# Attention over 64 heads on one core: score tiles spread over the whole head, their own three PSUM banks, and a new written-out order on all engines

## The reference, cut to what matters

```python
def ttt_filter(scores):
    int_scores = (jnp.abs(scores) * 1618.0).astype(jnp.int32)
    mod9 = int_scores % 9
    chaos = (mod9 == 0) | (mod9 == 3) | (mod9 == 6)
    return scores * jnp.where(chaos, 1 / PHI, 1.0)

def qrt_damping(x):
    return jnp.sin(C1 * x) * jnp.exp(-(x * x) / PHI) + jnp.cos(C2 * x)

scores = jnp.einsum('bhqd,bhkd->bhqk', q, k) / 8.0
attn = jax.nn.softmax(ttt_filter(scores), axis=-1)
attn = attn * qrt_damping(attn)
ctx = jnp.einsum('bhqk,bhkd->bhqd', attn, v)
```

## Time and profile before

| | |
|---|---|
| time, median of 3 runs | 7027.4 us (7016.34 to 7040.62) |
| profiled execution: its time / its span | 7039.49 us / 7037.8 us |
| busy in the span: PE, DVE, ACT, POOL | 81%, 64%, 60%, 39% |
| mean granted TensorE clock | 0.894 of full speed |

### The profile page before, as it was taken

The page is one execution under the profiler, slowest core; times in us unless marked ns, Lnnn a source line. Parts: engine busy times, 40 slices in busy tenths (PEclk is TensorE's granted clock), DMA queues, the critical chain, the costliest instruction groups (busy, mean ns, idle before and its releaser), DMA issues. The chain is left out here.

```text
span 7037.8 us, 110191 instructions
## 1 busy us (share of the span) xinstructions
PE 5716.5 (81%) x28905; PEld 3244.8 (46%) x28905; DVE 4477.5 (64%) x9249; ACT 4254.5 (60%) x7370; POOL 2765.9 (39%) x2640
## 2 busy tenths in 40 slices
PE   2788887887788787888788877788788699997999
PEld 1344443434444343444444334444444377775777
DVE  1766677677666667677766667667766555555443
ACT  1677777677777777777777777777777422222222
POOL 3444444444444444444444444444444301100111
PEclk9888889899888989888888999888888799998989
DMA  1000000000000000000000000000000000000000
GB/s 17 11 7 7 7 7 7 7 7 7 7 10 7 7 7 7 7 7 7 7 7 10 7 7 7 7 7 7 7 7 7 8 1 1 1 1 12 4 5 5
DMA packets 34512, 48.56 MB, mean 7 GB/s; under 512 B 24473, under 2 KB 24537, under 8 KB 34010
## 3 DMA queue, kind: packets, MB, share of 16 engines
q1 hardware_dynamic: 31962, 43.49, 2.4%
q0 software_dynamic: 2048, 0.14, 0.1%
HBM read 39.40 MB, written 4.19 MB: 6 GB/s over the span
## 5 line engine op out<-in xcount | busy, mean ns | idle before, releaser
L587 PE MATMUL banks<-ident,att 128*128 128x128 f32 x8192 | 1492.0, 313 | 644.9 <-DVE ag L523 633.2
L587 PEld LDWEIGHTS banks<-ident,att 128*128 128x128 f32 x8192 | 1044.0, 162 | 1483.8 <-DVE ag L523 1173.9
L388 POOL TENSOR_TENSOR sinb<-sinb,ag 128x512 f32<-128x512 f32 x1024 | 1289.4, 1274 | 1041.6 <-ACT sinb L453 1039.4
L615 PE MATMUL banks<-kT,qT 128*128 128x512 f32 x2048 | 1233.1, 687 | 344.1 <-DVE mx L550 189.8
L398 POOL TENSOR_SCALAR wgt<-wgt 128x512 f32<-128x512 f32 x1024 | 703.4, 687 | 1693.5 <-DVE wgt L516 1688.2
L489 DVE TENSOR_TENSOR work<-banks,work 128x512 f32<-128x512 f32 x1024 | 704.8, 690 | 907.2 <-ACT work L447 854.8
L653 PE MATMUL outp<-work,vo 128*64 128x512 f32 x2048 | 1105.8, 628 | 4.1 <-ACT att L435 4.1
L653 PE MATMUL outp<-sinb,vo 128*64 128x512 f32 x2048 | 1105.9, 628 | 0.0
L471 ACT ACTIVATE mag<-banks 128x512 f32<-128x512 f32 x1024 | 601.8, 594 | 552.7 <-PE banks L615 551.5
L464 ACT ACTIVATE work<-banks 128x512 f32<-128x512 f32 x1024 | 610.3, 596 | 372.9 <-PE banks L587 357.0
L453 ACT ACTIVATE sinb<-banks 128x512 f32<-128x512 f32 x1024 | 606.5, 597 | 312.8 <-PE banks L602 312.8
(11 more groups left out here) (200 smaller groups left out, 7252.1 us busy)
## 6 DMA issues: line engine op xcount, KB each, us to landing
xq<-xT_dram SPq DMA_DIRECT2D x64, 256.0 KB
xv<-xT_dram SPq DMA_DIRECT2D x64, 256.0 KB, 3.7
xT_dram<-xT SPq DMA_DIRECT2D x8, 256.0 KB, 2.9
out<-hres SPq DMA_DIRECT2D x8, 256.0 KB, 2.6
base<-in_L_tok_turns,idx POOLq DMA_INDIRECT x64, 2.3
wqk<-in_L_attn_Wq SPq DMA_DIRECT2D x64, 16.0 KB
wqk<-in_L_attn_Wk SPq DMA_DIRECT2D x64, 16.0 KB
wqk<-in_L_attn_bq SPq DMA_DIRECT2D x64, 0.2 KB
```

The source lines that it names most:

```text
L388: nc.gpsimd.tensor_tensor(sinb[:, k % RING], sinb[:, k % RING], ag[:, k], ALU.mult).then_inc(tmul, 1)
L587: mm = nc.tensor.matmul(bank[:, i * P:(i + 1) * P], att[:, p, 4 * half + i, kt * P:(kt + 1) * P], ident[:], is_transpose=True, start=(i == ...
L615: nc.tensor.matmul(score_bank(n), qT[:, p, (n // 2) * P:(n // 2 + 1) * P], kT[:, (n % 2) * 512:(n % 2 + 1) * 512], start=True, stop=True). ...
```

## The change

The tables hold other numbers, and the banks and two buffers are dealt out differently.

```diff
-        xq = sb("xq", [D + 1, S])
-        xv = sb("xv", [D + 1, S])
+        x = sb("x", [D + 1, S])
-        kT = sb("kT", [P, S])
+        kT = sb("kT", [P, 2, S])
...
-        SCORE = [5, 7, 9, 11] + list(range(12, 24))
-        ABS, RND, KEEP, FACT, FILT = (1, 1, 2, 2, 3)
-        PROJ, VAL = 24, 29 + STEPS
-        EXP = STEPS + 3
+        SCORE = [0, 1, 2, 5, 6, 13, 16, 19, 20, 23, 26, 27, 32, 33, 36, 40]
+        ABS, RND, FACT, FILT, BIAS = 1, 1, 2, 3, 4
+        EXP = [STEPS + o for o in [4, 5, 7, 8, 9, 10, 12, 16]]
...
         def score_bank(n):
-            return banks[:, n % 4]
-        def gauss_bank(d):
-            return banks[:, 4 + d % 3]
-        def sine_bank(k):
+            return banks[:, n % 3]
+        def turn_bank(k):
             return banks[:, 3 + k % 4]
...
-                wait(sp, projd, 2 * t)
+                if isinstance(t, int):
+                    wait(sp, projd, 2 * t)
+                else:
+                    wait(sp, vald, t - 2)
...
-                        if a in SCORE:
-                            n = SCORE.index(a)
-                            wait(pe, filtered, NTILE * g + n - 3)
-                            if n == 3:
-                                wait(pe, sined, NTILE * (g - 2) + 13)
...
-                        j = a - EXP - PACE
-                        if 0 <= j < TB:
-                            wait(pe, expd, TB * g + j + 1)
...
+                            wait(pe, filtered, NTILE * g + (n - 2 if n >= 3 else (0, -2, -1)[n]))
```

More of the change, by code:

```diff
@@ L351, in load_v @@
             def load_v(t):
-                wait(sp, vald, t)
-                sp.dma_start(xv[0:D, :], tokens(t)).then_inc(loadv, 16)
+                if isinstance(t, int) and t + 3 > NHEADS:
+                    wait(sp, vald, t)
+                else:
+                    wait(sp, projd, 2 * (t + 3))
+                sp.dma_start(x[0:D, :], tokens(t)).then_inc(loadv, 16)
             load_q(0)
             load_q(1)
+            load_q(2)
             load_v(0)
-            with sp.Fori(2, NHEADS) as t:
+            with sp.Fori(3, NHEADS) as t:
                 load_q(t)
-                load_v(t - 1)
+                load_v(t - 2)
+            load_v(NHEADS - 2)
             load_v(NHEADS - 1)
@@ L410, in projections @@
                 if c == 0:
[L411 removed]
+                    wait(act, qk, NTILE * (g - 1))
                 cols = slice(c * 512, (c + 1) * 512)
@@ L414, in projections @@
                 nc.scalar.activation(qT[rows, p, cols], outp[0:D], ACT.Copy, scale=QSCALE).then_inc(qk_sb, 1)
-                nc.scalar.activation(kT[rows, cols], outp[D:P], ACT.Copy).then_inc(qk_sb, 1)
+                nc.scalar.activation(kT[rows, p, cols], outp[D:P], ACT.Copy).then_inc(qk_sb, 1)
             projections(0, 0, 0)
@@ L422, in iteration @@
                     for c in range(2):
-                        if s == PROJ + EV + 2 * c and (not isinstance(t, int) or t + 1 < NHEADS):
+                        if s == PROJ[c] + EV and (not isinstance(t, int) or t + 1 < NHEADS):
                             projections(t + 1, 1 - par, c)
@@ L541, in iteration @@
                     for g, p, a in stages(t, par, s):
+                        if a - RND in SCORE:
+                            n = SCORE.index(a - RND)
+                            wait(dve, mags, NTILE * g + n + 1)
+                            wait(dve, filtered, NTILE * g + n - 3)
+                            nc.vector.tensor_scalar(wgt[:, n % 4], mag[:, n % 4], 1.0 / 6.0, ROUND,
+                                                    ALU.add, ALU.add).then_inc(rounded, 1)
+                            wait(dve, rounded, NTILE * g + n + 1)
+                            nc.vector.scalar_tensor_tensor(wgt[:, n % 4], wgt[:, n % 4], ROUND, mag[:, n % 4],
+                                                           ALU.subtract, ALU.is_gt).then_inc(kept, 1)
                         if a - FILT in SCORE:
                             n = SCORE.index(a - FILT)
-                            u, c = n // 2, n % 2
+                            u, cols = n // 2, slice(n % 2 * 512, (n % 2 + 1) * 512)
                             wait(dve, factor, NTILE * g + n + 1)
@@ L605, in iteration @@
                             mm.then_inc(nned, 1)
+                    for g, p, a in stages(t, par, s):
+                        if a in GAUSS:
+                            d = GAUSS.index(a)
+                            if d < 4:
+                                wait(pe, sined, NTILE * (g - 1) + 13 + d)
+                            else:
+                                wait(pe, agd, NTILE * g + d - 3)
+                            fill(g, p, turn_bank(d), d % TB, d // TB)
+                        if a in SINE:
+                            k = SINE.index(a)
+                            if k < 4:
+                                wait(pe, agd, NTILE * g + 13 + k)
+                            else:
+                                wait(pe, sined, NTILE * g + k - 3)
+                            fill(g, p, turn_bank(k), k % TB, k // TB)
                         if a in SCORE:
@@ L674, in iteration @@
                     for c in range(2):
-                        if s == PROJ + 2 * c and (not isinstance(t, int) or t + 1 < NHEADS):
+                        if s == PROJ[c] and (not isinstance(t, int) or t + 1 < NHEADS):
                             project(t + 1, 1 - par, c)
```

142 lines of the change are left out of this document (57 added, 85 removed).

## The result

| | before | changed |
|---|---|---|
| median | 7030.2 us | 6547.9 us (6538.8 to 6554.1, 4 runs) |
| ratio to before, 95% interval | | 0.9314 (0.9293 to 0.9335) |
| span of the profiled execution | 7037.8 us | 6537.1 us |
| mean granted clock | 0.894 | 0.918 |

What follows compares the result with a forecast made beforehand. Different engines were taken to bound each stretch in turn, with DVE full in the Gaussians and mostly idle in the waves. 29.0 + 28.6 + 14.9 = 72.5 us per head against 83.1 gave 6359 us, range 6120 to 6640.

Steps and rivals of the forecast that it cites:

- What bounds the kernel: Whole head, 83.1 us: no engine full throughout; DVE busy 38.0 of 40 us in Gaussians, only 10.3 of 26 in waves.
- Gaussians 29.0: Steps 11 to 28, seven score tiles left: ACT 27.4 us, DVE 25.4, plus 1.6 for waiting; bounds 27.4 and 32.
- Waves 28.6: Steps 28 to 43: 27.0 us, 1 for contention of DVE and POOL, some 0.6 of waiting; bounds 26 and 32.
- about 30 before: The forecast's length in us of the waves in the kernel before the change, set beside its 28.6.
- Exponentials 14.9: Steps 0 to 10 and the first fill: ACT 14.0 us, POOL 12.9 to 15.9; bounds 14.0 and 17.
- Edges and loads at nothing: Start and end of the kernel, both zero within 10 us; loads with one token buffer, 9 steps or more of cover.
- Rival 1: Engines near 80% full hand each wait on in order: 77 to 81 us a head, 6640 to 6900 us; chance 0.12.
- Rival 3: POOL products and DVE score work shut each other out: 17.8 us, up to 90.3 a head, 7480 us; chance 0.04.
- Rival 4: No change, from an unseen bound such as the clock at 0.50 through the Gaussians: 81 to 83 us a head; chance 0.04.
- Rival 2: Stretches melt together, only the fullest engine over the head counts: 64 to 68 us a head, 5820 to 6080 us; chance 0.06.

Runs made afterwards that it cites:

- old score steps on new banks: The changed kernel with its score tiles back at steps 5, 7, 9, 11 and 12 to 23, three score banks kept: 8008.4 us, ratio 1.1371.
- round late: The changed kernel with rounding and comparison one step later behind the absolute value, and factor, filter and bias one step later too: 6373.3 us, ratio 0.906.

## Why the prediction was right, and where it was off

The direction and the range held, and so did the main idea, that score work moved out of the Gaussians shortens the head. The terms did less well, and the sum came near because errors of both signs met in it. Step by step:

- *What bounds the kernel: DVE in the Gaussians, idle in the waves.* Right. The Gaussians fell from 41.3 to 27.2 us, and with the score tiles put back, and their banks, the time was 7060 us.
- *Gaussians 29.0, ACT the fullest.* 27.1 measured in the head read, 27.2 in the mean. That this is ACT's sum of 27.4 is luck. ACT had 25.0 us of work in 27.7, and a pair of square and exponential took 1.17 us (2832.89 to 2834.06) where 1.28 was counted. The fullest engine was DVE, with 27.0 of 27.7 where 25.4 was forecast: roundings to turns, a scaled row and two evacuations took 7.1 us where 4.5 stood for them. In the next head, which has no fold, both had 24.5 of 26.0. So the pairs came 1.7 us apart, as forecast, but paced by DVE.
- *Waves 28.6, contention about 1 us.* 28.8 in the head read, 29.0 in the mean: right as a sum. But "about 30 before" was not at the same marks: it ends at the table load of the exponentials, and so holds the last cosine and three sines, which the forecast counts with the exponentials. At one set of marks the waves were 26.5 and grew by 2.5. PE was to have no gaps and was busy 25.3 of 28.5 us. The price of contention in them alone was not measured.
- *Exponentials 14.9, bounds 14.0 and 17.* This is the mis-sized term; it measured 20.0. I summed the loads of ACT and POOL and said that POOL comes near ACT. What set the time was neither, but a queue on DVE: tiles 0 to 2 in consecutive steps, their three roundings and comparisons in line before the filter of tile 0, most of them lengthened beside the products that still run on POOL. I wrote of three score banks that the way from multiplication to filter fits "except at tiles 0 to 2, where it is in the 14.9". It wasn't: no part of the 14.9 held this wait, which is 3.9 us on PE. ACT itself had 13.7 us of work in 19.5, close to the 14.0 counted. In the means over the heads the stretch fell from 19.5 to 17.5 with the filter first and to 16.1 with the comparison in PSUM as well.
- *Edges and loads at nothing.* For the loads right: no wait for one stands among the waits of the 800 us. The edges were to be nothing within 10 us, and 23 of the 501 us between the two profiled spans lie outside the 63 intervals, 20 of them behind the last copy of the values. That end took 1499 to 1536 us in the other runs, with no order that I can see, so these 23 us are not shown to come from the change.
- *Rival 1, coupling costs more* was part of what happened, at one place. *Rival 3's* mechanism, the shut-out by the port, is real: 2.3 us of DVE per head came off the comparison when it was removed there. With the rounding's 3.7 us, which no run removed by itself, it is some 6 us and not 17.8. *Rival 4*: the granted clock rose, from 0.89 to 0.93 over the same 800 us. *Rival 2* did not come.

Summed by terms: 29.0 + 28.6 + 14.9 = 72.5 forecast, 27.1 + 28.8 + 20.0 = 75.9 in the head read. By the 63 intervals the mean is 75.5.

## What to carry to other kernels

Where four in-order engines share a pipeline, spread an engine's surplus over the stretch in which it is idle, and then ask at each place where three consecutive tiles start what the *first* one's last step is queued behind. Give an operation that waits for another engine a step more than its latency seems to need: rounding, and what follows it, one step later was worth 175 us, where the whole rearrangement brought 482. Work moved beside an engine that shares its SBUF port costs more than its duration; take an operand from PSUM where the data allow it (here they do not: the absolute value that the comparison needs lies in SBUF). And compare a stretch between runs over many periods, not in one.

## What the runs showed of the hardware that I had not expected

- A comparison with two SBUF operands beside a POOL product took up to 1.65 us for 0.69, a rounding up to 1.49 for 0.41, and the product up to 1.70 for 1.27. Both sides pay. With one of the comparison's operands in PSUM its mean was 0.688 us, and the product's 1.282 for 1.313.
- An operation on DVE that reads what the one before it wrote starts later: rounding to comparison of the same tile 0.46 us (2796.24 to 2796.70), of different tiles 0.33. Over a head that adds up to 2 us of DVE; whether they can be had back was not shown.
- With gaps of 1.6 to 1.8 us before score tiles the tile behind took 2.08 us, where one without such gaps took 1.13, and the granted clock was 0.78 in the mean of 800 us (old score steps on new banks).
- Before the last cosine of every second head ACT stood still for 2.1 to 2.5 us (in round late for 1.7 to 1.9) with nothing to wait for in the profile. The loop's body is two heads long; what the time is spent on was not tested.
